# A transformer block with self-attention, cross-attention and gated feed-forward: VectorE's step reordered, and the normalisation of x done by GpSimd

## What is computed

```python
def _ln(x, g, b):
    mu = mean(x); var = mean(square(x - mu))
    return (x - mu) * rsqrt(var + EPS) * g + b

def _attn(x, ctx, Wq, Wk, Wv, Wo, bo):          # 16 heads of 64
    q, k, v = x @ Wq, ctx @ Wk, ctx @ Wv
    attn = softmax(einsum(q, k) * 64 ** -0.5)
    return einsum(attn, v) @ Wo + bo

h = _ln(x, g1, be1);  x = _attn(h, h, Wq1, Wk1, Wv1, Wo1, bo1) + x
h = _ln(x, g2, be2);  x = _attn(h, context, Wq2, Wk2, Wv2, Wo2, bo2) + x
h = _ln(x, g3, be3);  y = h @ Wp + bp
a, gate = halves of y
x = a * gelu(gate) @ W2 + b2 + x
```

## Time and profile before

| | us |
|---|---|
| median of three runs | 3169.32 (3163.63 to 3170.73) |
| the profiled execution | 3167.35 |
| its span, first to last instruction | 3165.5 |
| PE busy | 2988.4 (94%) |
| DVE busy | 2364.2 (75%) |
| ACT busy | 1856.1 (59%) |
| POOL busy | 1265.0 (40%) |
| mean granted clock of PE | 0.991 |

### The profile page before, as it was taken

The page is one execution under the profiler, slowest core; times in us unless marked ns, Lnnn a source line. Parts: engine busy times, 40 slices in busy tenths (PEclk is TensorE's granted clock), DMA queues, the critical chain, the costliest instruction groups (busy, mean ns, idle before and its releaser), DMA issues. The chain is left out here.

```text
span 3165.5 us, 77555 instructions
## 1 busy us (share of the span) xinstructions
PE 2988.4 (94%) x25600; PEld 2601.8 (82%) x25600; DVE 2364.2 (75%) x4043; ACT 1856.1 (59%) x5615; POOL 1265.0 (40%) x783
## 2 busy tenths in 40 slices
PE   7999999999999998799999999999999969999999
PEld 6888888888888887688888888888888848888888
DVE  6777877777777776788888888888888856555654
ACT  6666666666666665566666666666666632233232
POOL 4444444444444444444444444444444420001100
PEclk9999999999999999899999999999999989999999
DMA  8887878788788887588778878878887850000100
GB/s 248 240 237 235 240 234 240 237 242 240 236 240 239 240 238 235 177 237 237 237 239 237 237 235 242 239 234 244 239 237 237 234 146 27 27 27 33 33 27 20
DMA packets 464422, 624.99 MB, mean 197 GB/s; under 512 B 57728, under 2 KB 397056, under 8 KB 464128
## 3 DMA queue, kind: packets, MB, share of 16 engines
q1 hardware_dynamic: 460256, 624.09, 66.3%
q10 hardware_dynamic: 4128, 0.41, 0.1%
HBM read 330.71 MB, written 293.60 MB: 197 GB/s over the span
## 5 line engine op out<-in xcount | busy, mean ns | idle before, releaser
L367 POOL TENSOR_TENSOR cross_probs<-cross_probs,cross_row_inv 128x1024 f32<-128x1024 f32 x256 | 484.7, 1893 | 652.2 <-DVE cross_row_inv L570 652.2
L367 POOL TENSOR_TENSOR self_probs<-self_probs,self_row_inv 128x1024 f32<-128x1024 f32 x256 | 484.8, 1894 | 642.7 <-DVE self_row_inv L570 642.7
L412 ACT ACTIVATE cross_probs<-cross_ps_s,cross_neg_max 128x256 f32<-128x256 f32 x1024 | 473.3, 472 | 139.3 <-DVE cross_blocks L562 69.1
L412 ACT ACTIVATE self_probs<-self_ps_s,self_neg_max 128x256 f32<-128x256 f32 x1024 | 472.9, 473 | 79.0 <-DVE self_neg_max L543 51.7
L543 DVE TENSOR_REDUCE self_neg_max<-self_ps_s 128x2 f32<-128x512 f32 x512 | 328.2, 682 | 141.7 <-PE self_ps_s L716 141.7
L543 DVE TENSOR_REDUCE cross_neg_max<-cross_ps_s 128x2 f32<-128x512 f32 x512 | 331.0, 683 | 113.0 <-PE cross_ps_s L716 112.1
L562 DVE STREAM_TRANSPOSE cross_blocks<-cross_probs 128x1024 f32<-128x1024 f32 x256 | 318.2, 1243 | 119.3 <-POOL cross_probs L367 108.1
L562 DVE STREAM_TRANSPOSE self_blocks<-self_probs 128x1024 f32<-128x1024 f32 x256 | 317.9, 1242 | 111.8 <-POOL self_probs L367 104.6
L464 ACT ACTIVATE self_qk_hi<-self_ps_qk 128x512 fp32r<-128x512 f32 x256 | 153.2, 598 | 233.0 <-PE self_ps_s L716 153.3
L464 ACT ACTIVATE cross_qk_hi<-cross_ps_qk 128x512 fp32r<-128x512 f32 x256 | 152.7, 596 | 209.0 <-PE cross_ps_s L716 151.4
L976 ACT ACTIVATE ff_u_hi<-ff_gated 128x512 fp32r<-128x512 f32 x128 | 80.9, 632 | 301.5 <-PE ff_ps_y L1116 214.2
(11 more groups left out here) (166 smaller groups left out, 9579.6 us busy)
## 6 DMA issues: line engine op xcount, KB each, us to landing
self_turns<-self_blocks SPq DMA_DIRECT2D x1024, 128.0 KB, 2.8
self_probs_t<-self_turns SPq DMA_DIRECT2D x256, 512.0 KB, 4.4
cross_turns<-cross_blocks SPq DMA_DIRECT2D x1024, 128.0 KB, 2.8
cross_probs_t<-cross_turns SPq DMA_DIRECT2D x256, 512.0 KB, 4.4
self_xt<-in_x SPq DMA_DIRECT2D x32, 256.0 KB, 6.3
self_xres<-in_x SPq DMA_DIRECT2D x32, 256.0 KB, 2.7
after_self_attention<-yout SPq DMA_DIRECT2D x32, 256.0 KB, 2.4
cross_xt<-after_self_attention SPq DMA_DIRECT2D x32, 256.0 KB, 6.2
```

The source lines that it names most:

```text
L367: pool.tensor_tensor(tile, tile, scale, ALU.mult).then_inc(probs_ready, 1)
L412: last = act.activation(probs[:, slot % 2, h, t], scores[:, slot % 2, h, t], ACT.Exp, bias=neg_max[:, slot % 2, i:i + 1], accum_out=row_su ...
```

## The change

In DVE's step the reciprocal of the older pair and `o_lo` now come ahead of the older pair's transpose. At p = 6 `output` comes ahead of the younger pair's transpose. DVE no longer adds EPS and no longer normalises x: POOL does both with three operations, an add of two elements with a tile that holds EPS, a subtraction of the mean and a multiplication by `rstd` over 128 x 512, between its passes over the probabilities at the end of p = 2. The stages' waits follow: POOL waits for the mean and variance instead of `var_eps`, and for the earlier transposes of x before it overwrites `xnorm`.

```diff
--- before.py
+++ after.py
@@ -168,6 +168,7 @@
         ident = sb("ident", [P, P], F32)
         pause = sb("pause", [P, 1], F32)
         minus_half = sb("minus_half", [P, TT], F32)
+        eps = sb("eps", [P, TT], F32)
 
 
         xt = sb("xt", [P, TT, DIM], F32)
@@ -224,6 +225,7 @@
         meanvar_ready = sem("meanvar_ready")
         var_ready = sem("var_ready")
         rstd_ready = sem("rstd_ready")
+        centred = sem("centred")
         xnorm_ready = sem("xnorm_ready")
         h_transposed = sem("h_transposed")
         h_t_ready = sem("h_t_ready")
@@ -333,13 +335,26 @@
         def _(pool):
             make_identity(nc, pool, ident, ident_made)
             pool.memset(minus_half[:], -0.5).then_inc(half_made, 1)
-            pool.wait_ge(half_made, 1)
+            pool.memset(eps[:], EPS).then_inc(half_made, 1)
+            pool.wait_ge(half_made, 2)
 
             def norm_power(b):
-                pool.wait_ge(var_ready, b + 1)
+                pool.wait_ge(meanvar_ready, TT * (b + 1))
                 if counts(c := b):
                     pool.wait_ge(xnorm_ready, c)
+                pool.tensor_tensor(var_eps[:], meanvar[:, :, 1], eps[:], ALU.add).then_inc(var_ready, 1)
+                pool.wait_ge(var_ready, b + 1)
                 pool.tensor_tensor(rstd[:], var_eps[:], minus_half[:], ALU.pow).then_inc(rstd_ready, 1)
+
+            def norm_apply(b):
+                pool.wait_ge(rstd_ready, b + 1)
+                if counts(c := b):
+                    pool.wait_ge(h_transposed, c)
+                mean = meanvar[:, :, 0:1].to_broadcast([P, TT, DIM])
+                pool.tensor_tensor(xnorm[:], xt[:], mean, ALU.subtract).then_inc(centred, 1)
+                pool.wait_ge(centred, b + 1)
+                pool.tensor_tensor(xnorm[:], xnorm[:], rstd[:].unsqueeze(2).to_broadcast([P, TT, DIM]),
+                                   ALU.mult).then_inc(xnorm_ready, 1)
 
             def low_h(b):
                 pool.wait_ge(h_hi_ready, b + 1)
@@ -374,12 +389,14 @@
                     residual(b - 1)
                 if part in (FIRST, LOOP) and p == 2:
                     norm_power(b + 1)
+                    norm_apply(b + 1)
                 if part in (FIRST, LOOP) and p == 6:
                     low_h(b + 1)
                     if cross:
                         low_context(b + 1)
 
             norm_power(0)
+            norm_apply(0)
             low_h(0)
             if cross:
                 low_context(0)
@@ -507,17 +524,6 @@
                 nc.vector.memset(pause[:], 0.0)
                 for t in range(TT):
                     nc.vector.bn_aggr(meanvar[:, t], stats[:, t]).then_inc(meanvar_ready, 1)
-                dve.wait_ge(meanvar_ready, TT * (b + 1))
-                nc.vector.tensor_scalar(var_eps[:], meanvar[:, :, 1], EPS, None, ALU.add).then_inc(var_ready, 1)
-
-            def norm_apply(b):
-                dve.wait_ge(rstd_ready, b + 1)
-                if counts(c := b):
-                    dve.wait_ge(h_transposed, c)
-                for t in range(TT):
-                    last = nc.vector.tensor_scalar(xnorm[:, t], xt[:, t], meanvar[:, t, 0:1], rstd[:, t:t + 1],
-                                                   ALU.subtract, ALU.mult)
-                last.then_inc(xnorm_ready, 1)
 
             def context_copy(b):
                 dve.wait_ge(c_transposed, b + 1)
@@ -578,22 +584,22 @@
 
             def step(b, p, part):
                 g = PAIRS * b + p
-                if alive(part, p, TURNED):
-                    turn(b, p)
                 if alive(part, p, NORMED):
                     inverse(b, p)
                 if alive(part, p, PROJECTED):
                     low_o(b, p)
+                if alive(part, p, TURNED):
+                    turn(b, p)
                 if part != DRAIN:
                     low_parts(g, p)
+                if part != FIRST and p == 6:
+                    output(b - 1)
                 if alive(part, p + 1, TURNED):
                     turn(b, p + 1)
                 if alive(part, p + 1, NORMED):
                     inverse(b, p + 1)
                 if part in (FIRST, LOOP) and p == 2:
                     norm_stats(b + 1)
-                if part != FIRST and p == 6:
-                    output(b - 1)
                 if alive(part, p, SCORES):
                     maxima(g - SCORES, (p - SCORES) % 2, 0)
                 if part != DRAIN:
@@ -607,11 +613,8 @@
                 if alive(part, p + 1, SCORES):
                     for h in range(2):
                         maxima(g + 1 - SCORES, (p + 1 - SCORES) % 2, h)
-                if part in (FIRST, LOOP) and p == 2:
-                    norm_apply(b + 1)
 
             norm_stats(0)
-            norm_apply(0)
             if cross:
                 context_copy(0)
             for i, w in enumerate(("wq", "wk", "wv")):
```

## The result

The changed kernel takes 3159.42 us in the median (3152.14 to 3164.05, 20 runs), the kernel before, beside it, 3170.73 (3163.63 to 3177.99, 20 runs): a ratio of 0.9963, interval 0.9955 to 0.997. That is faster, by 11.3 us, less than half of the 23 us forecast. The profiled executions are 5.7 us apart, 3161.7 us (span 3159.9) against 3167.35 (3165.5).

What follows compares the result with a forecast made beforehand. TensorE, busy 2988.4 of 3165.5 us, bounds the kernel, so only its standing still counts. Gains of cross 19 + 6, self 22 - 25 and first steps 1 make 23 us off 3167.35: 3144.4, predicted 3145 us, range 3095 to 3183.

Steps and rivals of the forecast that it cites:

- Part 1: Reciprocal and o_lo ahead of DVE's older transpose: 19 us gained at p = 4 in cross, 22 us in self.
- Part 2: POOL normalises x instead of DVE: cost 0, hidden by POOL's idle time between p = 2 and p = 4.
- Part 3: Output's sum ahead of p = 6's younger transpose: transpose 1.20 later in self, 0.93 in cross, delaying p = 0's loads.
- the sum of p = 0 in cross: At p = 0 in cross: 1.38 - 0.55 - 0.65 = 0.18 us per sequence gained, 6 us over 31 sequences.
- the rest of p = 0: At p = 0 in cross: the chain after c_lo, hidden by the wait on c_lo, so no cost.
- self's loss: At p = 0 in self: later loads make 0.8 us of new wait over 31 sequences, 25 us lost.
- the 1 us of the first steps: In the first steps: a shorter queue takes 1 us off.
- A: Rival at p = 0: the loads land in time despite later issue, 3099 us; chance 0.18.
- B: Rival at p = 0's second load, both stages: it lands later still, 3207 us at another 1 us; chance 0.14.
- C: Rival: the older transpose and a POOL pass block each other, transposes of 2 us, 3270 us; chance 0.06.
- D: Rival: o_lo still waits, since ACT and not DVE is last; given no chance of its own.
- The rule of the Trainium skill: At p = 0 in cross: DVE and GpSimd lock shared ports, c_hi could delay c_lo by 0.3, some 6 us more.

Runs made afterwards that it cites:

- The first experiment's kernel: The changed kernel with output's sum put back behind the younger pair's transpose at p = 6; 3098.84 us, ratio 0.9785.
- the fifth kernel: The changed kernel with SyncE's wait for y's store and the residual's load moved behind p = 0's loads of probs_t; 3099.87 us, ratio 0.9769.
- part 1 alone: The kernel before with only the reciprocal and o_lo moved ahead of the older transpose; 3114.39 us, ratio 0.9827.
- part 2 alone: The kernel before with only POOL's three operations normalising x in place of DVE's; 3125.75 us, ratio 0.9866.

## Why the prediction was right in direction and wrong in size

**Part 1, right.** Waits on `o_lo` below 15 us: 12.2. p = 4 in cross 0.62 shorter with the transposes at S + 6.1: 0.58 and S + 6.09, because the chain through the late transpose and ACT's exponentials ran as worked out. Cross 18 us for 19; self (0.68 + 0.09) x 31 = 24 for 22; p = 2 in cross 1 us lost for 0.

**Part 2, right.** Cost 0 in the steady steps. The two passes take 1.04 each, under the 1.3 taken and inside its bounds, and the add 0.20; x is ready 5.4 us early. Only the first x of a stage comes later from POOL: TensorE waits 8.9 us for it in self, before 7.4, and 1.1 in cross, where before no such wait is listed.

**Part 3, right in mechanism, wrong in price.** The younger transpose ends 1.20 later in self, as forecast, and 0.82 in cross against 0.93. The second load is issued 1.21 and 0.98 after its old place (medians over the sequences) and takes 6.25 and 6.35 us to land, before 6.33 and 6.09, for 6.4 in the prediction: its own condition, 0.4 us either way, holds. The new waits came where it put them. The step that failed is the sum of p = 0 in cross, "0.18 x 31 = 6 us" gained, "1.38 - 0.55 - 0.65". Measured: 0.16 x 31 = 5 us lost. Its terms, per sequence:

| term | forecast | measured |
|---|---|---|
| wait on `o_lo` gone | -1.38 | -1.35 (10.30 - 8.95) |
| `c_lo` | +0.55 | +0.68 |
| the loads | +0.65 | +0.81 |
| the rest of p = 0 | 0 | +0.18 |
| shorter step | 0 | -0.16 |
| p = 0 | -0.18 | +0.16 |

The measured terms are differences of step lengths: `c_lo` from the start of V's matmuls (S + 2.08 at the median for S + 1.40), the loads from the stretch of the last matmuls (2.69 from their start to the next step, 1.88 where nothing is waited for), and the rest is what is left of 10.46 - 8.79. The idle time at the loads is 0.65 a sequence in cross (18.7 us over 29 steady sequences), just as forecast; the other 0.16 is the slow restart. The prediction had read that restart in its first part ("idle time and 0.2 of slow restart") and counted it for the waits removed, but left it out of the waits added, in self too: there its "0.8 of new wait" stands against 0.74 of idle time and 0.97 by the step's length (10.32 - 9.35). For `c_lo` it took 0.05 where the row's 0.37 of idle time costs 0.68. That makes 0.13 + 0.16 in cross and 0.17 in self, 0.46 x 31 = 14 us. Of the 0.2 of a restart, 0.16 is a matter of counting: the view's idle time starts at the end of the last matmul, 0.28 after its start, where the next would have started after 0.12.

The rest of p = 0, 6 us, is the term that the prediction put at nothing because `c_lo` "hides the rest of p = 0's chain". The matmuls between `c_lo` and the loads run longer at p = 0 than at p = 6 with no stop listed, most of all the younger pair's q and k, 1.47 us against 1.34. The first experiment's kernel, without the wait on `c_lo`, has the same 1.47. Its cause stays open.

**The sum.** Against the forecast of -23: p = 0 in cross 11 us worse; self's loss 29 for 25; self's gain 2 better; p = 4 and p = 2 in cross 2 worse; p = 6 in cross 5 better, unforeseen; the two long stops at the stages' last sequences 6 worse, unforeseen; the 1 us of the first steps not seen. In the profiled pair that is -6. The medians say -11.3; the executions of either kernel lie 12 us and more apart, and no finer account than that of the profiled pair can be given.

**The rivals.** A (the loads land in time) is out by 45 us of waits at p = 0. B (they land later still, beyond the later issue) is out: the time to landing moved by -0.1 us in self and +0.3 in cross, less than the 0.4 that it needed. The prediction named the queue's order (stored, landed, residual, loads) and didn't ask what it was worth: by the fifth kernel 60 us, as much as part 3 costs. C (transpose and POOL block each other) is out: 222 of the 512 transposes of both stages now run beside a POOL pass for over 0.3 us, before none, and they take as long as the others, 1.23 us. Their group in the kernel after, against 1243 ns:

```profile
L568 DVE STREAM_TRANSPOSE cross_blocks<-cross_probs 128x1024 f32<-128x1024 f32 x256 | 315.4, 1232 | 10.3 <-DMA cross_turns<-cross_blocks 9.4 <-POOL cross_probs L382 0.6
```

D is out by the rows on `o_lo`. The rule of the Trainium skill on the two engines' common ports (SBUF — State Buffer, "SBUF: two separate sides") would have had `c_hi` hold `c_lo` up by 0.3. DVE does seem to wait: `c_hi` begins at 2072.59, beside `h_lo`, and ends at 2073.66, 0.28 behind the end of `h_lo`. But `c_lo` begins at 2073.52, while `c_hi` still runs, 0.14 behind `h_lo` (2073.38), and takes 0.73 as before: here POOL isn't held up, and the rows give nothing of the rule's 6 us. The first experiment's kernel shows that it can be. There `h_lo` is already done when `c_hi` begins, and `c_lo` begins 0.08 behind `c_hi`:

```profile
2021.01 0.42 DVE L542 TENSOR_TENSOR cross_c_hi<-cross_c_t,cross_c_hi 64x256 fp32r<-64x256 f32 x1
2021.09 0.95 POOL L367 TENSOR_TENSOR cross_c_lo<-cross_c_t,cross_c_hi 128x256 fp32r<-128x256 f32 x1
```

`c_hi` takes 0.42 instead of 1.07 and `c_lo` 0.95 instead of 0.73, and so, within 0.02 us, in all its steady sequences. Where the two overlap by more than the last 0.14 us, the one that began second is stretched, be it DVE's operation or POOL's. One sequence of the kernel before has it this way round too (`c_lo` 1.0 us long at 2392.0), which the prediction overlooked.

## What to carry to other kernels

A wait costs its idle time and the restart after it. Whoever prices removed waits by the step's length must price new ones so too, and the more so where many small ones are added (here some 90 at p = 0, about 21 us more than their idle time). When a move delays a transfer, look at what stands between its trigger and its issue in the in-order queue: one load that nobody needed soon, kept behind a wait for a store, decided about 60 us here. And the parts of an edit that touch one chain don't add up: 54 and 42 us alone were 69 together.

## What the runs showed that was not expected

TensorE's pace differs between kernels also where no stop is listed. In cross at p = 6 before, the projection's second matmul came 0.19 us after the first (2029.99 - 2029.80) instead of 0.12, too little for the view of waits to list. `o_lo` had ended at 2029.72, only 0.08 ahead of the first, in a step that the prediction called free of stops; part 1 alone removes the 0.07, part 2 alone doesn't. With the rest of that row of twelve it makes 0.09 of the 0.16 by which p = 6 is shorter. PE, kernel before, then after:

```profile
2029.80 0.36 PE L749 MATMUL cross_ps_y<-cross_hi_wo,cross_o_hi 128*128 128x256 f32 x1
2029.99 0.28 PE L749 MATMUL cross_ps_y<-cross_hi_wo,cross_o_lo 128*128 128x256 f32 x1
```

```profile
2066.68 0.28 PE L752 MATMUL cross_ps_y<-cross_hi_wo,cross_o_hi 128*128 128x256 f32 x1
2066.80 0.28 PE L752 MATMUL cross_ps_y<-cross_hi_wo,cross_o_lo 128*128 128x256 f32 x1
```

The other 0.07 is the pace of matmuls that wait for nothing: a quarter of V in cross goes at 118.1 ns a matmul at the median before and at 114.7 after, at a mean granted clock of 0.991 and 0.990. Part 1 alone has 118.1, part 2 alone 114.7, so it comes with part 2; what in it (its longer list of tiles, POOL's or DVE's traffic) wasn't tried and stays open.

A pass of POOL over 128 x 512 with one operand spread from a value per row took 1.04 us, where `h_lo` of the same size with two full inputs took 1.27.
